# Row flows with ScalarE's copies of older pairs and TensorE's linear layer at the head of each turn

## The chip, the cores and the metric

The kernel runs on one core of a Trainium2 chip. Its engines, TensorE (PE), VectorE (DVE), ScalarE (ACT), GpSimd (POOL) and SyncE (SP, which only issues transfers), each work through their own list of instructions in order and meet at semaphores. The metric is the device time in microseconds of one execution; lower is better. PEclk in the profile is the clock that TensorE was granted, as a share of 2.4 GHz; its other level, 1.2 GHz, reads 0.50.

## The reference

Four layers, each a graph step and a feed-forward step, on x with 2708 rows of 256. What matters here is the beginning of each graph step, which works row by row:

```python
x = x + _L0_gnn_ref(_layernorm(x), adj, L0_gnn_W)     # data = [y, A@y/deg]; data @ W.T
x = x + _L0_ffn_ref(_layernorm(x), ...)               # 32 experts, argmax
x = x + _L1_gnn_ref(_layernorm(x), adj, ...)          # h1 = y @ W1 + b1; three rounds of A @ h
x = x + _L1_ffn_ref(_layernorm(x), ...)               # 8 experts, top 2, weights
x = x + _L2_gnn_ref(_layernorm(x), adj, adj, ...)     # h2 = tanh(y @ W_proj + b); A' @ (h2 @ W_gcn)
# layer 3 and the other feed-forward steps are not touched
```

So before every product with the adjacency matrix each row is normed and multiplied by a 256 x 256 (in layer 0 a 256 x 512) matrix.

## The kernel before, in words

The 2708 rows are padded to 22 tiles of 128, taken as 11 pairs (PR = 11). The three row flows, classes S0, C0 and C1, run the pairs through a chain of steps on several engines. S0 makes [y W] of layer 0 at the program's start; C0 adds the first experts' gathered rows to x and makes the first linear layer of layer 1; C1 adds the weighted rows of the second experts and makes the projection, tanh and second product of layer 2. For each pair:

- VectorE: take (add gathered rows to x, L615 or L657 and L662), statistics (L362), aggregate (L365, semaphore ag);
- ScalarE: root as Ln and Exp (L369, L371, semaphore le; in C1 it is GpSimd's, L375 and L377);
- VectorE: a Newton step, four small instructions (L382 to L390, semaphore rs);
- ScalarE: the two norms (L395, semaphore y);
- TensorE: four transposes (L437, semaphore t);
- ScalarE: high fp16 half (L444, in C1 L747, semaphore xh); VectorE: low half (L412, L785, semaphore xl);
- TensorE: the linear layer in triples of fp16 products (L260 to L262, semaphore mm; in C0 two more for the bias, L577 and L578; in C1 a projection for every second pair first, L756 and L761 its tanh and high half);
- ScalarE: copy of the result as high half HAh (L516, L600 and L603, L766, semaphore hh); VectorE: low half HAl (L531, L628, L775, semaphore hl), in S0 also the residual sum L530 (semaphore xa).

In S0 x itself has to be turned first: TensorE transposes it (L469, semaphore tx) and ScalarE copies it (L502, semaphore xe).

The flows are software pipelines written out by hand: in turn i each engine does step k for pair i - lag(k). The order inside a turn is the order of the lines, and since an engine works in order, an instruction that waits holds up all behind it. Each stage behind a flow begins with work that waits for the flow's last pairs: P0 (L1010 on ScalarE, then L1029 on VectorE), P1 (L881 on TensorE), P2 (L1353 on VectorE). VectorE's order, GpSimd's and SyncE's are the same in both kernels.

Of the kernel before, what the change touches and what calls it, by code (L numbers as in the profile page):

```python
# [14 lines left out]
D = 256  # L15
# [57 lines left out]
def build(nc, io):  # L73
    ctx = ExitStack()
    with ctx:
# [327 lines left out]
        def pair(i):  # L403
            return slice(2 * i, 2 * i + 2)

        def bank2(b):
            return ps[:, b, :].rearrange("p (a d) -> p a d", a=2)
# [40 lines left out]
        class S0:  # L448
# [7 lines left out]
            def pe(self, pe):  # L456
                s = self.st
                w = [z[:, 0:4 * D].rearrange("p (s f d) -> p f s d", s=2, f=FT) for z in (WH, WLo)]
                pe.wait_ge(LC["id"], 16)

                def turn_in(j):
                    for c, (a, b) in enumerate(XCH):
                        if j == a:
                            pe.wait_ge(LC[f"x{c}"], 16)
                    s.wait(pe, "xe", j - 1)
                    for a in range(2):
                        for f in range(FT):
                            q = 2 * a + f
                            mm = pe.transpose(ps[:, 2 + j % 2, q * P:(q + 1) * P],  # L469
                                              xT[:, f, (2 * j + a) * P:(2 * j + a + 1) * P], ident[:, :])  # L470
                    mm.then_inc(s["tx"], 1)

                def linear(j):
                    if j == 0:
                        after(pe, W[0])
                    s.wait(pe, "xl", j + 1)
                    s.wait(pe, "xa", j - 1)
                    s.wait(pe, "hl", j - 1)
                    for a in range(2):
                        out = ps[:, 4 + 2 * (j % 2) + a, :].rearrange("p (s d) -> p s d", s=2)  # L480
                        for f in range(FT):
                            mm = mm3(pe, out, xtp[:, j % 2, 0, 2 * a + f, :], xtp[:, j % 2, 1, 2 * a + f, :],
                                     w[0][:, f], w[1][:, f], start=f == 0, stop=f == FT - 1)
                    mm.then_inc(s["mm"], 1)

                turn_in(0)
                for i in range(PR + 3):
                    if i + 1 < PR:
                        turn_in(i + 1)
                    if 0 <= i - 1 < PR:  # L490
                        turns(pe, s, i - 1, (i - 1) % 2)
                    if 0 <= i - 3 < PR:
                        linear(i - 3)

            def act(self, act):
                s = self.st
                act.preload_act_table_set("natural_log_exp_and_others")
                act.wait_ge(LC["v"], 3)
                for i in range(PR + 4):
                    if i < PR:  # L500
                        s.wait(act, "tx", i + 1)
                        act.activation(x[:, pair(i), :], bank2(2 + i % 2), ACT.Copy).then_inc(s["xe"], 1)  # L502
                        s.wait(act, "ag", i + 1)
                        root_act(act, 2 * (i % 3), 2, s)
                    if i == 1:
                        W[0].act(act)
                    if 0 <= i - 1 < PR:
                        act.wait_ge(s["xe"], s.at("xe") + i)
                        normals(act, s, i - 1)
                    if 0 <= i - 2 < PR:  # L510
                        high_half(act, s, i - 2, (i - 2) % 2)
                    j = i - 4
                    if 0 <= j < PR:
                        s.wait(act, "mm", j + 1)
                        b = 4 + 2 * (j % 2)
                        act.activation(HAh[:, pair(j), 0:D], ps[:, b:b + 2, D:2 * D], ACT.Copy).then_inc(s["hh"], 1)  # L516

            def pool(self, pool):
                W[0].pool(pool)
# [25 lines left out]
        class C0:  # L545
# [18 lines left out]
            def pe(self, pe):  # L564
                s = self.st
                after(pe, self.experts, W[1])
                a0, n0 = _ROWS["L1_b1"]

                def linear(j):
                    s.wait(pe, "xl", j + 1)  # L570
                    s.wait(pe, "hl", j - 1)
                    for a in range(2):
                        out = ps[:, 4 + j % 2, a * D:(a + 1) * D]
                        for f in range(FT):
                            mm3(pe, out, xtp[:, j % 2, 0, 2 * a + f, :], xtp[:, j % 2, 1, 2 * a + f, :],
                                WH[:, f * D:(f + 1) * D], WLo[:, f * D:(f + 1) * D], start=f == 0)
                        pe.matmul(out, ones16[:, 0:P], rowh[:, a0:a0 + n0], start=False, stop=False)  # L577
                        mm = pe.matmul(out, ones16[:, 0:P], rowl[:, a0:a0 + n0], start=False, stop=True)  # L578
                    mm.then_inc(s["mm"], 1)

                for i in range(PR + 3):
                    if 0 <= i - 1 < PR:
                        turns(pe, s, i - 1, 2 + (i - 1) % 2)
                    if 0 <= i - 3 < PR:
                        linear(i - 3)

            def act(self, act):
                s = self.st
                for i in range(PR + 4):
                    if i < PR:  # L590
                        s.wait(act, "ag", i + 1)
                        root_act(act, 2 * (i % 3), 2, s)
                    if 0 <= i - 1 < PR:
                        normals(act, s, i - 1)
                    if 0 <= i - 2 < PR:
                        high_half(act, s, i - 2, 2 + (i - 2) % 2)
                    j = i - 4
                    if 0 <= j < PR:
                        s.wait(act, "mm", j + 1)
                        act.activation(nrow[:, pair(j), :], bank2(4 + j % 2), ACT.Copy).then_inc(s["nn"], 1)  # L600
                        for a in range(2):
                            t = 2 * j + a
                            op = act.activation(HAh[:, t, 0:D], ps[:, 4 + j % 2, a * D:(a + 1) * D], ACT.Identity,  # L603
                                                scale=dinv[:, t:t + 1])
                        op.then_inc(s["hh"], 1)

            def dve(self, v):
                s = self.st
# [58 lines left out]
        class C1:  # L667
# [28 lines left out]
            def pe(self, pe):  # L696
# [26 lines left out]
                    mm.then_inc(s["mm"], 1)  # L723

                for i in range(PR + 8):
                    if 0 <= i - 1 < PR:
                        turns(pe, s, i - 1, 2 + (i - 1) % 2)
                    j = i - 3
                    if 0 <= j < PR and (j % 2 == 1 or j == PR - 1):
                        project(j // 2)  # L730
                    if 0 <= i - 7 < PR:
                        linear(i - 7)

            def act(self, act):
                s = self.st
                after(act, *self.before)
                b0 = _COLS["b_proj"]
                for i in range(PR + 9):
                    if 0 <= i - 1 < PR:
                        normals(act, s, i - 1)  # L740
                    j = i - 2
                    if 0 <= j < PR:
                        g = j // 2
# [6 lines left out]
                    if 0 <= j < PR and (j % 2 == 1 or j == PR - 1):  # L750
# [4 lines left out]
                        for m in range(FT):  # L755
# [4 lines left out]
                        s.wait(act, "mm", 2 * g - 2)  # L760
                        act.activation(self.h2[:, g % 2, 0, :, 0:n, :], self.th[:, :, 0:n * P].rearrange("p m (t c) -> p m t c", c=P),  # L761
                                       ACT.Copy).then_inc(s["h2h"], 1)
                    j = i - 8
                    if 0 <= j < PR:
                        s.wait(act, "mm", j + 1)
                        act.activation(HAh[:, pair(j), 0:D], bank2(6 + j % 2), ACT.Copy).then_inc(s["hh"], 1)  # L766

            def dve(self, v):
                s = self.st
# [1985 lines left out]
```

## Time and profile before

| what | value |
|---|---|
| median of 3 runs | 2637.11 us (2624.55 to 2652.12) |
| the profiled execution's own time | 2658.08 us |
| its span (first to last instruction) | 2655.9 us |
| busy: TensorE, VectorE, ScalarE, GpSimd | 2075.8, 1573.1, 1082.8, 497.0 us |
| mean granted clock of TensorE | 0.895 |
| S0 | 0 to 76 us |
| C0 | first gather issued at 428.35, first take at 437.31, last low half ends at 515.5 |
| C1 | first load issued at 1373.43, first take at 1376.83, last low half ends at 1456.7 |

Busy time is the time in which an engine had an instruction running, and says nothing of why it stood in between. For that the timeline gives, in brackets, how long the engine was idle before an instruction and which instruction's end released it. Instructions on one engine overlap a little: a ScalarE copy that takes 0.58 us lets the next start 0.48 us after its own start, so that lengths of a turn are measured from start to start.

### The profile page before, as it was taken

The numbers are of one execution on the slowest core, as the hardware profiler recorded it, in microseconds if no ns is written. First come the engines' busy times: TensorE is split into PE (matmuls) and PEld (weight loads), VectorE is DVE, ScalarE is ACT, GpSimd is POOL, SyncE is SP. The second block draws the span as 40 slices with busy tenths as digits, with TensorE's granted clock in tenths as the row PEclk, the third lists the DMA queues.
The fourth block names the chain that finished last, engine by engine and source line by source line (L and its number), as shares of the span: only waits on it lengthen the run. The fifth ranks groups of instructions, "written<-read, shape, count | busy, mean of one in ns | idle before, by whom it ended". The sixth has DMA issues, their size and how long they took to land. (4 is left out here: it accounts for less than half of the span.)

```text
span 2655.9 us, 46982 instructions
## 1 busy us (share of the span) xinstructions
PE 2075.8 (78%) x17062; PEld 1393.9 (52%) x17062; DVE 1573.1 (59%) x2950; ACT 1082.8 (41%) x2336; POOL 497.0 (19%) x464
## 2 busy tenths in 40 slices
PE   5899284899999999358856899178954899997597
PEld 3688152588888888346643677166732222222243
DVE  4666654454545566753346897633364899996633
ACT  5454264421212233345534775445543123233344
POOL 0000453000000000374430233544410000000200
PEclk9899597699999999769988899599966999998689
DMA  4899368055455555332223673511230332321000
GB/s 134 256 357 303 103 142 240 15 199 237 198 239 201 238 234 235 109 110 65 65 89 105 168 184 84 160 57 61 67 106 34 125 112 78 90 77 51 16 0 42
DMA packets 211970, 357.69 MB, mean 135 GB/s; under 512 B 18680, under 2 KB 165753, under 8 KB 197050
## 3 DMA queue, kind: packets, MB, share of 16 engines
q1 hardware_dynamic: 189118, 310.39, 34.7%
q0 software_dynamic: 13152, 35.93, 5.2%
q10 hardware_dynamic: 9504, 8.65, 1.0%
q8 instruction: 135, 2.21, 0.3%
q14 instruction: 61, 0.50, 0.1%
HBM read 291.81 MB, written 63.12 MB: 134 GB/s over the span
## 5 line engine op out<-in xcount | busy, mean ns | idle before, releaser
L881 PE MATMUL ps<-R,BIG 128*128 128x256 f16 (+1 forms) x1936 | 532.5, 275 | 23.1 <-DVE BIG L1357 13.4
L882 PE MATMUL ps<-R,BIG 128*128 128x256 f16 x1936 | 528.7, 273 | 0.0
L883 PE MATMUL ps<-R,BIG 128*128 128x256 f16 (+1 forms) x1936 | 528.6, 273 | 0.0
L1799 DVE TENSOR_TENSOR X<-X 128x512 f16<-128x512 f32 (+1 forms) x152 | 84.4, 556 | 332.3 <-ACT X L1780 318.7
L2265 PE MATMUL ps<-BIG 128*64 128x452 f32 x1056 | 233.7, 564 | 35.2 <-DVE BIG L2380 30.8
L881 PEld LDWEIGHTS ps<-R,BIG 128*128 128x128 f16 x1936 | 187.9, 97 | 58.4 <-DVE BIG L1357 13.7
L260 PE MATMUL ps<-X,BIG 128*128 128x128 f16 x904 | 189.6, 227 | 25.3 <-issue 20.0
L882 PEld LDWEIGHTS ps<-R,BIG 128*128 128x128 f16 x1936 | 190.4, 98 | 23.2
L883 PEld LDWEIGHTS ps<-R,BIG 128*128 128x128 f16 x1936 | 188.3, 97 | 26.4
L262 PE MATMUL ps<-X,BIG 128*128 128x128 f16 x904 | 191.0, 227 | 6.6 <-issue 6.5
L261 PE MATMUL ps<-X,BIG 128*128 128x128 f16 x904 | 186.3, 222 | 11.5 <-issue 11.5
L2380 DVE SCALAR_TENSOR_TENSOR BIG<-BIG 128x904 f32<-128x904 f32 x176 | 192.4, 1155 | 4.8 <-DVE BIG L2375 4.0
L1775 ACT ACTIVATE X<-ps,cols 128x128 f32<-128x128 f32 x452 | 137.7, 380 | 126.8 <-PE ps L262 59.6
L2300 ACT ACTIVATE BIG<-X,BIG 128x64 f32 (+1 forms) x264 | 70.2, 337 | 260.8 <-PE ps L2271 260.8
L2265 PEld LDWEIGHTS ps<-BIG 128*64 128x64 f32 x1056 | 64.8, 137 | 201.7 <-issue 119.9
L1676 POOL DMA_INDIRECT X<-rows_split,idxg x152 | 149.7, 985 | 109.3 <-issue 35.4
L1738 PE MATMUL ps<-BIG,X 128*128 x452 | 157.3, 383 | 11.1 <-issue 3.7
L437 PE MATMUL ps<-ident,yln 128*128 128x128 f32 x176 | 42.5, 387 | 123.6 <-ACT yln L395 118.7
L1692 POOL DMA_INDIRECT expert_out<-X,idxs x100 | 98.9, 989 | 188.2 <-DVE X L1805 173.5
L881 PE MATMUL ps<-XX,BIG 128*128 128x256 f16 x484 | 132.2, 273 | 0.3 <-DVE XX L1216 0.3
L883 PE MATMUL ps<-XX,BIG 128*128 128x256 f16 x484 | 131.9, 273 | 0.0
L882 PE MATMUL ps<-XX,BIG 128*128 128x256 f16 x484 | 131.9, 273 | 0.0
(347 smaller groups left out, 4599.7 us busy)
## 6 DMA issues: line engine op xcount, KB each, us to landing
BIG<-adj_split SPq DMA_DIRECT2D x66, 1408.0 KB, 12.8
BIG<-in_adjT SPq DMA_DIRECT2D x42, 1408.0 KB, 11.1
adj_split<-BIG SPq DMA_DIRECT2D x22, 1408.0 KB
BIG<-in_adj SPq DMA_DIRECT2D x22, 1408.0 KB, 6.1
BIG<-in_adjT SPq DMA_DIRECT2D x66, 452.0 KB, 3.3
BIG<-in_f SPq DMA_DIRECT2D x88, 256.0 KB, 3.0
BIG<-expert_out SPq DMA_DIRECT2D x44, 256.0 KB, 2.9
rows_split<-row ACTq DMA_DIRECT2D x66, 128.0 KB, 3.4
```

The source lines that it names most:

```text
L260: pe.matmul(out, ah, bh, start=start, stop=False)
L261: pe.matmul(out, ah, bl, start=False, stop=False)
L262: return pe.matmul(out, al, bh, start=False, stop=stop)
L881: pe.matmul(out[:, 0:n], pr[:, 0, k, :], h[:, k, 0:n], start=start, stop=False)
L882: pe.matmul(out[:, 0:D], pr[:, 0, k, :], l[:, k, 0:D], start=False, stop=False)
L883: return pe.matmul(out[:, 0:n], pr[:, 1, k, :], h[:, k, 0:n], start=False, stop=stop)
L1676: pool.indirect_dma_start(xg[:, j % 4, :], None, xrows[:, :], bass.IndirectOffsetOnAxis(ap=idxg[:, j:j + 1], axis=0)).then_inc(s[f"g{j % 4 ...
L1692: pool.indirect_dma_start(ys_dram[:, :], bass.IndirectOffsetOnAxis(ap=idxs[:, j:j + 1], axis=0), yo[:, j % 4, :], None).then_inc(s[self.ou ...
L1738: pe.matmul(ps[:, 4 + u, :].rearrange("p (h d) -> p h d", h=2), hh[:, u, t, :], w, start=t == 0, stop=False)
L1775: op = act.activation(hact[:, u, t, :], ps[:, 2 + u, t * P:(t + 1) * P], self.func, bias=cols[:, dyn(e[j] * HT + (self.b1 + t), 1)], scale=sc)
L2265: pe.matmul(ps[rs, 2 * (h // 2) + c, 0:CW], self.G[:, u, h * HF:(h + 1) * HF], self.PT[:, u, h, cs], start=start, stop=stop)
L2380: op = v.scalar_tensor_tensor(self.PT[:, u, h, :], Q[h // 2][:, h % 2, :], Z[:, dyn(HEADS * k + h, 1)], self.MK[:, u, :], ALU.max, ALU.mult)
```

## The change

ScalarE's turn is rearranged in all three flows. Before, it did root, norms, high half of pair i-2, then the copy HAh of pair i-4. Now it does the copy HAh, the high half, then the root and the norms; in S0 the copy of x comes first, for pair i+1 in place of pair i, with the copy of pair 0 ahead of the loop. In C1 the copy HAh of pair i-8 is first and the norms are last, behind high half and tanh. TensorE's turn has the linear layer (in C1 projection and linear layer) in front of the transposes of the norms instead of behind them. The lags stay.

```diff
@@ S0.pe
                     if i + 1 < PR:
                         turn_in(i + 1)
+                    if 0 <= i - 3 < PR:
+                        linear(i - 3)
                     if 0 <= i - 1 < PR:
                         turns(pe, s, i - 1, (i - 1) % 2)
-                    if 0 <= i - 3 < PR:
-                        linear(i - 3)
@@ S0.act
+                def rows_in(i):
+                    s.wait(act, "tx", i + 1)
+                    act.activation(x[:, pair(i), :], bank2(2 + i % 2), ACT.Copy).then_inc(s["xe"], 1)
+
+                rows_in(0)
                 for i in range(PR + 4):
+                    if i + 1 < PR:
+                        rows_in(i + 1)
+                    j = i - 4
+                    if 0 <= j < PR:
+                        s.wait(act, "mm", j + 1)
+                        b = 4 + 2 * (j % 2)
+                        act.activation(HAh[:, pair(j), 0:D], ps[:, b:b + 2, D:2 * D], ACT.Copy).then_inc(s["hh"], 1)
+                    if 0 <= i - 2 < PR:
+                        high_half(act, s, i - 2, (i - 2) % 2)
                     if i < PR:
-                        s.wait(act, "tx", i + 1)
-                        act.activation(x[:, pair(i), :], bank2(2 + i % 2), ACT.Copy).then_inc(s["xe"], 1)
                         s.wait(act, "ag", i + 1)
                         root_act(act, 2 * (i % 3), 2, s)
...
-                    if 0 <= i - 2 < PR:
-                        high_half(act, s, i - 2, (i - 2) % 2)
-                    j = i - 4
-                    if 0 <= j < PR:
-                        s.wait(act, "mm", j + 1)
-                        b = 4 + 2 * (j % 2)
-                        act.activation(HAh[:, pair(j), 0:D], ps[:, b:b + 2, D:2 * D], ACT.Copy).then_inc(s["hh"], 1)
@@ C0.pe
+                    if 0 <= i - 3 < PR:
+                        linear(i - 3)
                     if 0 <= i - 1 < PR:
                         turns(pe, s, i - 1, 2 + (i - 1) % 2)
-                    if 0 <= i - 3 < PR:
-                        linear(i - 3)
@@ C0.act (root and norms moved behind; what stands in j's block is unchanged)
-                    if i < PR:
-                        s.wait(act, "ag", i + 1)
-                        root_act(act, 2 * (i % 3), 2, s)
-                    if 0 <= i - 1 < PR:
-                        normals(act, s, i - 1)
-                    if 0 <= i - 2 < PR:
-                        high_half(act, s, i - 2, 2 + (i - 2) % 2)
                     j = i - 4
...
+                    if 0 <= i - 2 < PR:
+                        high_half(act, s, i - 2, 2 + (i - 2) % 2)
+                    if i < PR:
+                        s.wait(act, "ag", i + 1)
+                        root_act(act, 2 * (i % 3), 2, s)
+                    if 0 <= i - 1 < PR:
+                        normals(act, s, i - 1)
@@ C1.pe
-                    if 0 <= i - 1 < PR:
-                        turns(pe, s, i - 1, 2 + (i - 1) % 2)
...
                     if 0 <= i - 7 < PR:
                         linear(i - 7)
+                    if 0 <= i - 1 < PR:
+                        turns(pe, s, i - 1, 2 + (i - 1) % 2)
@@ C1.act
-                    if 0 <= i - 1 < PR:
-                        normals(act, s, i - 1)
+                    j = i - 8
+                    if 0 <= j < PR:
+                        s.wait(act, "mm", j + 1)
+                        act.activation(HAh[:, pair(j), 0:D], bank2(6 + j % 2), ACT.Copy).then_inc(s["hh"], 1)
...
-                    j = i - 8
-                    if 0 <= j < PR:
-                        s.wait(act, "mm", j + 1)
-                        act.activation(HAh[:, pair(j), 0:D], bank2(6 + j % 2), ACT.Copy).then_inc(s["hh"], 1)
+                    if 0 <= i - 1 < PR:
+                        normals(act, s, i - 1)
```

How ScalarE's list stands in the middle of S0 (x is written at X, HAh is R, the high half xt), one turn and the beginning of the next, before:

```order
L369 ACTIVATE nrt<-mvt,eps 128x2
L371 ACTIVATE nrt<-nrt 128x2
L395 ACTIVATE yln<-X,nrt 128x256 x2
L444 ACTIVATE xt<-ps 128x512
L516 ACTIVATE R<-ps 128x2x256
L502 ACTIVATE X<-ps 128x512
```

and in the changed kernel, where L501 is the copy of x and L511 the copy HAh:

```order
L501 ACTIVATE X<-ps 128x512
L511 ACTIVATE R<-ps 128x2x256
L444 ACTIVATE xt<-ps 128x512
L369 ACTIVATE nrt<-mvt,eps 128x2
L371 ACTIVATE nrt<-nrt 128x2
L395 ACTIVATE yln<-X,nrt 128x256 x2
```

Read as a ring the two lists differ only in the order of L444 and the copy HAh. What moved is which pairs meet: the three copies now stand in front of the wait for the aggregate of the turn whose pairs they serve, and the copy of x is one pair ahead.

TensorE's list in S0, with the first linear layer (twelve products in triples, of which the first triple and the last product are shown). Before, the transposes of the norms (L437) of pair 2 stood ahead of it:

```order
L469 MATMUL ps<-ident,X 128x128 x4
L437 MATMUL ps<-ident,yln 128x128 x4
L260 MATMUL ps<-WH,xt 128x512
L261 MATMUL ps<-WLo,xt 128x512
L262 MATMUL ps<-WH,xt 128x512
```

and now, at the second linear layer, they stand behind the products, with the next transposes of x (L469) behind them:

```order
L262 MATMUL ps<-WH,xt 128x512
L437 MATMUL ps<-ident,yln 128x128 x4
L469 MATMUL ps<-ident,X 128x128 x4
L260 MATMUL ps<-WH,xt 128x512
L261 MATMUL ps<-WLo,xt 128x512
```

So L437, which waits for ScalarE's norms, no longer holds up the linear layer of an older pair.

ScalarE's list in C1, a turn without tanh, one with it, and the next norms, in the changed kernel (L747 is now the copy HAh, L754 the high half, L763 tanh, L768 its high half; in the kernel before the norms L395 open a turn and L766, the copy HAh, ends it):

```order
L395 ACTIVATE yln<-X,nrt 128x256 x2
L747 ACTIVATE R<-ps 128x2x256
L754 ACTIVATE XX<-ps 128x2x2x128
L763 ACTIVATE XX<-ps,cols 128x512 x2
L768 ACTIVATE XX<-XX 128x1024
L395 ACTIVATE yln<-X,nrt 128x256 x2
```

The norms of a pair now come behind tanh, which waits for TensorE's projection.

## Rows read from the trace of the kernel before

**Rows 1.** Stretches: us, then each engine's busy us (instructions), PEclk, DMA share, GB/s.
```profile
28.00:60.00 32.00, 21.03 (x113) 11.29 (x110) 19.32 (x66) 17.28 (x41) 0.00 (x0) 1.00 0.06 20
428.00:455.00 27.00, 3.58 (x15) 2.62 (x16) 9.23 (x34) 6.23 (x16) 11.37 (x12) 0.51 0.99 395
455.00:480.00 25.00, 18.67 (x83) 10.01 (x82) 13.02 (x47) 13.14 (x32) 7.57 (x8) 0.57 0.25 83
480.00:507.00 27.00, 21.88 (x92) 11.34 (x90) 14.07 (x47) 12.77 (x30) 1.90 (x2) 0.50 0.04 10
1400.00:1456.00 56.00, 38.47 (x226) 23.89 (x224) 33.05 (x87) 28.88 (x50) 4.73 (x10) 0.84 0.41 106
```

**Rows 2.** Waits in S0, 26 to 76: waiter, releaser, us, times, longest.
```profile
DVE X L530 <- ACT R L516: 22.2, 11, 3.1
```

**Rows 3.** Timeline, one turn of S0: start, us, engine, line, op, [idle before, releaser].
```profile
50.36 0.69 DVE L530 TENSOR_TENSOR X<-X,ps 128x512 f32<-128x512 f32 x1 [2.18 <-ACT R L516]
...
53.09 0.29 ACT L369 ACTIVATE nrt<-mvt,eps 128x2 f32<-128x2 f32 x1 [2.27 <-DVE mvt L365]
...
53.53 0.16 DVE L390 SCALAR_TENSOR_TENSOR nrt<-mvt,nrt 128x2 f32<-128x2 f32 x1
...
53.77 1.09 ACT L395 ACTIVATE yln<-X,nrt 128x256 f32<-128x256 f32 x2 [0.15 <-DVE nrt L390]
...
54.77 0.57 ACT L444 ACTIVATE xt<-ps 128x512 f16<-128x512 f32 x1
...
55.25 0.58 ACT L516 ACTIVATE R<-ps 128x512 f16<-128x512 f32 x1
```

**Rows 4.** Timeline, TensorE in the same turn of S0.
```profile
49.42 0.66 PE L437 MATMUL ps<-ident,yln 128*128 128x128 f32 x4 [1.82 <-ACT yln L395]
...
49.91 0.38 PE L260 MATMUL ps<-WH,xt 128*128 128x512 f16 x1
...
52.50 0.60 PE L469 MATMUL ps<-ident,X 128*128 128x128 f32 x4
```

**Rows 5.** Timeline, S0: first, seventh and last residual sum; ScalarE's next stage.
```profile
28.37 0.69 DVE L530 TENSOR_TENSOR X<-X,ps 128x512 f32<-128x512 f32 x1 [3.15 <-ACT R L516]
...
61.36 0.69 DVE L530 TENSOR_TENSOR X<-X,ps 128x512 f32<-128x512 f32 x1 [2.17 <-ACT R L516]
...
74.84 2.54 ACT L1010 ACTIVATE BIG<-BIG 128x2816 f16<-128x2816 f32 x1
...
74.97 0.69 DVE L530 TENSOR_TENSOR X<-X,ps 128x512 f32<-128x512 f32 x1 [2.05 <-ACT R L516]
```

**Rows 6.** Timeline, one turn of C0.
```profile
473.49 0.88 DVE L628 SCALAR_TENSOR_TENSOR R<-ps,dinv,R 128x256 f16<-128x256 f32 x2 [2.86 <-ACT R L603]
...
476.54 0.29 ACT L369 ACTIVATE nrt<-mvt,eps 128x2 f32<-128x2 f32 x1 [3.09 <-DVE mvt L365]
...
476.97 0.16 DVE L390 SCALAR_TENSOR_TENSOR nrt<-mvt,nrt 128x2 f32<-128x2 f32 x1
...
479.12 0.83 ACT L603 ACTIVATE R<-ps,dinv 128x256 f16<-128x256 f32 x2
...
479.99 0.88 DVE L628 SCALAR_TENSOR_TENSOR R<-ps,dinv,R 128x256 f16<-128x256 f32 x2 [2.86 <-ACT R L603]
```

**Rows 7.** Timeline, C0: takes of gathered rows, pairs 2 and 4.
```profile
446.14 0.69 DVE L615 SCALAR_TENSOR_TENSOR X<-BIG,X 128x512 f32<-128x512 f32 x1 [3.56 <-DMA BIG<-expert_out,posu]
...
454.75 0.69 DVE L615 SCALAR_TENSOR_TENSOR X<-BIG,X 128x512 f32<-128x512 f32 x1 [2.31 <-DMA BIG<-expert_out,posu]
```

**Rows 8.** Timeline, C0: take of the last pair, last low half.
```profile
493.79 0.42 DVE L617 SCALAR_TENSOR_TENSOR X<-BIG,X 128x256 f32<-128x256 f32 x1
...
514.61 0.88 DVE L628 SCALAR_TENSOR_TENSOR R<-ps,dinv,R 128x256 f16<-128x256 f32 x2 [2.67 <-ACT R L603]
```

**Rows 9.** Waits in C1, 1385 to 1460: waiter, releaser, us, times, longest.
```profile
DVE R L775 <- ACT R L766: 20.5, 9, 5.9
```

**Rows 10.** Timeline, the first work of the stage behind C1.
```profile
1456.58 3.08 DVE L1353 SCALAR_TENSOR_TENSOR BIG<-BIG 128x2816 f32<-128x2816 f32 x1
```

## The prediction

> **What bounds the kernel now.** I read the page first for where the time is, then the stretches, then the waits and the timelines of the three flows that are edited: S0 (from the start to 76 us), C0 (428 to 515) and C1 (1373 to 1457). Together they are some 240 of 2656 us; nothing else is touched. In the stretches the reader is to see that no engine is full there: in S0 TensorE is busy for 21.0 of 32 us, VectorE 19.3, ScalarE 17.3; in C0 it is 18.7, 13.0 and 13.1 of 25 [rows 1]. So it is no engine's work that sets the pace but waits in a circle. The waits name it: VectorE stood 22.2 us, all 11 times, for ScalarE's last copy of a turn, L516 [rows 2].
>
> The timeline shows the circle. VectorE's turn opens with the residual sum L530 at 50.36, held until that copy, and ends the part that matters (the aggregate for the root) when ScalarE starts L369 at 53.09: 2.73 us. ScalarE had nothing it could do ahead of this, since the root stands in front of its other work. Then root, norms, and the copies of older pairs follow, L516 from 55.25 to 55.83: 2.74 us [rows 3]. Only now may VectorE's next turn open. 2.73 + 2.74 is 5.47, and the measured turn is (61.36 - 28.37) / 6 = 5.50 us [rows 5]: the two engines run strictly one after the other. C0 is the same: VectorE 473.49 to 476.54 (3.05), ScalarE 476.54 to 479.95 (3.41), turn 6.50 [rows 6].
>
> **The change part by part.** No instruction is added or taken away. Moved are the copies (L516, L444; in S0 also the copy of x one turn ahead) to the head of ScalarE's turn, and TensorE's linear layer in front of the transposes.
>
> *ScalarE's copies first.* The copy that VectorE waits for is now done before ScalarE asks for the next aggregate, so VectorE's turn i can run beside ScalarE's root and norms of turn i-1. The circle above is cut. What is late next is the longest of these, for S0:
> - VectorE's own turn, 50.36 to 53.69: 3.33 us [rows 3].
> - ScalarE's own: root 0.68 (53.09 to 53.77), norms 1.00, three copies at 0.48 start to start: 3.12 us [rows 3].
> - TensorE's own: 2.59 for the linear layer (49.91 to 52.50) and 0.49 for each of two groups of transposes: 3.57 us [rows 4].
> - A new circle through both: ScalarE's turn now opens with the copy of the next x, which waits for its transposes; these stand on TensorE behind the last turn's transposes of the norms; and those wait for ScalarE's norms at the end of its turn. Its length: transposes 0.60 [rows 4], three copies 1.44, root 0.68, norms 1.09 [rows 3], the transposes of the norms 0.49 [rows 4], and three hand-overs that I put at 0.05 each (L516 ends at 55.83; the sum of both halves above leaves 0.03 for one): 4.45 us.
>
> So the S0 turn becomes 4.45, and six turns from 28.37 to 61.36 save 6 x 1.05 = 6.3. In the drain, 61.36 to 74.97 (13.6 for four turns) [rows 5], the transposes of x are over and TensorE's 2.59 + 0.49 = 3.08 is left: 12.3, which saves 1.3. For the filling I take another 1.4, bounded by nothing and a turn and a half. S0: **-9**, bounds -6 and -13.
>
> *TensorE's linear layer first.* Alone it would save nothing: it fills, with work that is ready, the 1.82 us that TensorE stood before L437 [rows 4], and without it the new circle would be longer by 2.59. I count it inside the 4.45.
>
> *C0.* There is no copy of x, so no new circle of that kind. VectorE's own turn is 473.49 to 477.13, 3.64; ScalarE's 3.41 [rows 6]; TensorE's is 18.67 / 25 x 6.50 = 4.85 at the clock of that stretch, 0.57 [rows 1], and some 2.4 at 1.00. Here the clock decides. Between 480 and 507 it is 0.50, the lower level of 1.2 GHz, with a wait before the transposes in each turn; in S0, also with a wait of 1.82 us in each turn, it stays at 1.00, 2.4 GHz [rows 1, 4]. After the change TensorE at the lower level has work for 4.85 in a turn that nothing else holds above 3.64, so it runs without a break, and I expect the upper level after about one turn; then it stands idle 3.64 - 2.4 = 1.2 us in each turn, less than the 1.82 us in S0 at which the upper level held. From the fifth take at 454.75 to the last at 493.79 there are six turns, 39.0 us [rows 7, 8]: one at 4.85 and five at 3.64 make 23.1, saving 16. The drain of 21.7 us behind the last take [rows 8] has five turns; at the upper level ScalarE without the root needs 3.41 - 0.63 = 2.8 for each, 14 together, -7.7; since the clock may rise late, I take half, -4. C0: **-20**, bounds -10 (lower level throughout, six turns of 4.85 = 29.1, drain as now) and -24.
>
> [...]
>
> *The gathers of C0.* Moving VectorE forward asks for gathered rows sooner. The takes of pairs 2 and 4 waited for them, 8.61 us for two turns, 4.3 a turn, while the DMA engines were 99% busy with the next stage's loads up to 455; behind it the share is 0.25 and 0.04 [rows 1, 7]. The loads don't depend on VectorE, so they are over at the same time, and I charge nothing after 455 and gain nothing before.
>
> *C1.* It had the same wait, 20.5 us in 9 times for L766 [rows 9]. In S0 I cut 9 of 22.2. Here ScalarE's tanh, now in front of the norms, waits for TensorE's projection, so part of the wait only moves; I take three tenths: **-6**, bounds 0 and -12.
>
> *What carries on.* S0's end is followed by ScalarE's L1010 at once (74.84) [rows 5], and C1's by VectorE's L1353 at 1456.58 [rows 10]: the stages behind start when the flows end, and so shift whole.
>
> Sum: -9 - 20 - 6 = -35. The profiled execution took 2658.1, so it would be 2623; it is 21 above the median of three, 2637.1, and against the median the forecast is **2602**.
>
> **The rivals.**
> - *The clock stays low in C0 and partly in C1.* C0 -10, C1 -4, S0 -9: -23, 2614. For it: 0.50 through the 27 us from 480 [rows 1]. Against: TensorE had a wait in each turn there, and at the lower level it now has none. 0.20.
> - *The gain is given back behind the flows.* If the stage after S0 is held by its transfers and not by the flow's end, S0's 9 are lost: -26, 2611. Against: L1010 follows at once [rows 5]. 0.12.
> - *Slower: TensorE never gets its clock in S0.* The linear layer and the transposes come in another rhythm; if the clock stayed at 1.2 GHz, TensorE's turn would be 2 x 3.57 = 7.14: six turns 42.8 instead of 33.0, +9.8, and the drain 4 x 6.16 = 24.6 instead of 13.6, +11. C0 -10. C1 had 38.5 busy at a mean clock of 0.84 [rows 1]; all at the lower level that is 38.5 x 0.84 x 2 = 65 in a stretch of 56, +9. Together +20, 2657. It decides from where TensorE's turn at the granted clock passes 5.50, which needs the lower level. Against it: the first linear layers still follow each other closely. 0.08.
>
> That the edit doesn't do what it says is not in question: it is an order written out, and the two orders differ as described.
>
> **How the numbers follow.** The forecast has 0.60, the rivals 0.20, 0.12 and 0.08. Low end: all bounds, -13 - 24 - 12 = -49, 2588, and 8 for the spread of a median (the three runs lie within 2625 to 2652), 2580. High end: the first rival, 2614, and 14 for that spread, 2628. About 1% (26 us) is what a measurement of this kernel can tell from no change. Faster by more than that means under 2611: three quarters of the forecast, half of the next two: 0.60. Slower by more than 1% is most of the last case: 0.06. Within 1%: 0.34.
>
> **What would show it.** In S0: turns of about 4.45 between two residual sums, VectorE's wait for the HAh copy gone, TensorE waiting less than 1 us for the norms, the next stage's first L1010 near 66. In C0: turns near 3.64 and PEclk over 0.9 from about 460; if turns are 4.85 with 0.50, the first rival holds. In C1: the last turns closer, the end 6 us sooner relative to the first take. It would be wrong if the flows shorten and the stages behind them lengthen by as much.

## The result and the profile after

| | before | changed |
|---|---|---|
| median | 2641.41 us (4 runs, 2624.55 to 2652.12) | 2601.06 us (4 runs, 2585.35 to 2605.20) |
| profiled execution, its span | 2658.08, 2655.9 us | 2605.20, 2603.0 us |
| S0, start to end of its last low half | 76.3 us | 61.5 us |
| C0, first take to end of the last low half | 78.2 us | 57.4 us |
| C1, the same | 79.8 us | 73.1 us |

The ratio is 0.983, with a 95% interval from 0.9802 to 0.9857: the changed kernel is 40 us faster. In the profiled executions the three flows together are 14.8 + 20.8 + 6.7 = 42.3 us shorter, and that is where the gain is. The profiled pair differs by 52.9, and the other 10.6 lie in stages that are not edited: 0.8 between S0 and C0, 5.5 between C0's end and C1's first take (861.3 us before, 855.8 after), and 4.3 behind C1. The long stretch between C0 and C1 varies that much by itself: it took 839 to 841 us in each of four kernels on another chip, and on a third chip 838 us in one execution and 856 to 859 us in three others.

S0 in the changed kernel, timeline of one turn (start, us, engine, line, op, [idle before, releaser]). L501 is the copy of x, L511 the copy HAh, L535 the residual sum that was L530; these answer to [rows 3, 4].

```profile
31.96 0.60 ACT L501 ACTIVATE X<-ps 128x512 f32<-128x512 f32 x1 [1.18 <-PE ps L469]
...
32.45 0.59 ACT L511 ACTIVATE R<-ps 128x512 f16<-128x512 f32 x1
...
33.08 0.69 DVE L535 TENSOR_TENSOR X<-X,ps 128x512 f32<-128x512 f32 x1 [0.83 <-ACT R L511]
...
33.41 0.31 ACT L369 ACTIVATE nrt<-mvt,eps 128x2 f32<-128x2 f32 x1
...
33.85 1.08 ACT L395 ACTIVATE yln<-X,nrt 128x256 f32<-128x256 f32 x2
...
34.98 0.66 PE L437 MATMUL ps<-ident,yln 128*128 128x128 f32 x4 [0.47 <-ACT yln L395]
...
35.48 0.60 PE L469 MATMUL ps<-ident,X 128*128 128x128 f32 x4
...
36.11 0.60 ACT L501 ACTIVATE X<-ps 128x512 f32<-128x512 f32 x1 [1.18 <-PE ps L469]
...
37.23 0.69 DVE L535 TENSOR_TENSOR X<-X,ps 128x512 f32<-128x512 f32 x1 [0.83 <-ACT R L511]
```

VectorE's wait of 2.18 us is down to 0.83, and ScalarE's wait for the aggregate (2.27 before L369) is gone. Two other waits now stand in the turn: ScalarE's of 1.18 for the transposes of x, which is new, and 0.47 that is left of TensorE's 1.82 for the norms. They lie on the circle of the forecast, and it can be added up from start to start: L437 to L469 0.50, to L501 0.63, three copies to L369 1.45, to L395 0.44, to L437 1.13, together 4.15. That is the turn.

The waits of S0, 26 to 67, answer to [rows 2], where VectorE's were 22.2 us:

```profile
DVE X L535 <- ACT R L511: 8.0, 9, 1.3
ACT X L501 <- PE ps L469: 5.9, 5, 1.2
PEld ps L437 <- ACT yln L395: 5.8, 6, 1.0
...
PE ps L437 <- ACT yln L395: 2.8, 6, 0.5
```

The first, seventh and last residual sum, and the next stage's first work, for [rows 5]:

```profile
24.77 0.69 DVE L535 TENSOR_TENSOR X<-X,ps 128x512 f32<-128x512 f32 x1 [2.34 <-ACT R L511]
...
48.78 0.68 DVE L535 TENSOR_TENSOR X<-X,ps 128x512 f32<-128x512 f32 x1
...
60.07 2.54 ACT L1015 ACTIVATE BIG<-BIG 128x2816 f16<-128x2816 f32 x1
60.21 0.69 DVE L535 TENSOR_TENSOR X<-X,ps 128x512 f32<-128x512 f32 x1 [1.30 <-ACT R L511]
```

C0, the low halves (L633, was L628) and the last take, for [rows 6 to 8]:

```profile
446.03 0.88 DVE L633 SCALAR_TENSOR_TENSOR R<-ps,dinv,R 128x256 f16<-128x256 f32 x2
...
450.82 0.88 DVE L633 SCALAR_TENSOR_TENSOR R<-ps,dinv,R 128x256 f16<-128x256 f32 x2 [1.14 <-ACT R L601]
...
455.60 0.88 DVE L633 SCALAR_TENSOR_TENSOR R<-ps,dinv,R 128x256 f16<-128x256 f32 x2 [1.14 <-ACT R L601]
...
460.39 0.88 DVE L633 SCALAR_TENSOR_TENSOR R<-ps,dinv,R 128x256 f16<-128x256 f32 x2 [1.14 <-ACT R L601]
...
463.96 0.88 DVE L633 SCALAR_TENSOR_TENSOR R<-ps,dinv,R 128x256 f16<-128x256 f32 x2
464.76 0.41 DVE L622 SCALAR_TENSOR_TENSOR X<-BIG,X 128x256 f32<-128x256 f32 x1
...
467.58 0.87 DVE L633 SCALAR_TENSOR_TENSOR R<-ps,dinv,R 128x256 f16<-128x256 f32 x2
```

The stretches, for [rows 1] (us, busy us of PE, PEld, DVE, ACT, POOL, then PEclk, DMA share, GB/s):

```profile
24.00:46.00 22.00, 19.64 (x108) 10.53 (x106) 16.57 (x56) 15.93 (x39) 0.00 (x0) 1.00 0.31 83
440.00:450.00 10.00, 9.70 (x41) 4.95 (x41) 9.11 (x34) 6.53 (x18) 5.66 (x6) 0.50 0.43 150
450.00:460.00 10.00, 10.00 (x44) 5.50 (x43) 7.02 (x24) 6.79 (x19) 3.78 (x4) 0.50 0.18 52
460.00:465.00 5.00, 5.00 (x37) 3.03 (x34) 4.47 (x15) 4.58 (x13) 0.00 (x0) 0.91 0.10 26
465.00:480.00 15.00, 13.70 (x108) 9.19 (x107) 10.06 (x34) 11.01 (x26) 0.00 (x0) 1.00 0.00 1
```

Here the two views must be read together. Three turns of C0 are 4.79 us long, with TensorE busy all 10.00 us of a stretch at the lower level; the next two are 3.57 and 3.62, with the clock at 0.91 and then 1.00. The lists of instructions are the same in both. What changed is the clock, and with it VectorE's wait of 1.14 for the copy HAh is gone.

C1's waits, 1338 to 1410, answer to [rows 9] (20.5 us there; L780 was L775, L747 was L766), and the start of the stage behind to [rows 10]:

```profile
ACT R L747 <- PE ps L262: 14.7, 7, 4.3
...
DVE R L780 <- ACT R L747: 10.4, 7, 4.2
```

```profile
1407.96 6.08 DVE L1358 SCALAR_TENSOR_TENSOR BIG<-BIG 128x2816 f32<-128x2816 f32 x2
```

### The profile page after: what moved, and what is told of

Read it like the earlier page. It is cut to its first block and busy times, and to the rows that moved or that the text cites. A ratio compares the mean times of both kernels' runs of the same rounds, so it can differ in the third digit from the quotient of the medians.

```text
span 2603.0 us, 46982 instructions
## 1 busy us (share of the span) xinstructions
PE 2067.1 (79%) x17062; PEld 1388.7 (53%) x17062; DVE 1575.1 (61%) x2950; ACT 1080.4 (42%) x2336; POOL 495.7 (19%) x464
## 5 line engine op out<-in xcount | busy, mean ns | idle before, releaser
L886 PE MATMUL ps<-R,BIG 128*128 128x256 f16 (+1 forms) x1936 | 532.5, 275 | 23.1 <-DVE BIG L1362 13.4
L260 PE MATMUL ps<-X,BIG 128*128 128x128 f16 x904 | 189.6, 227 | 17.3 <-issue 11.5
L888 PEld LDWEIGHTS ps<-R,BIG 128*128 128x128 f16 x1936 | 188.3, 97 | 26.3
L2305 ACT ACTIVATE BIG<-X,BIG 128x64 f32 (+1 forms) x264 | 70.2, 337 | 261.3 <-PE ps L2276 261.3
L1743 PE MATMUL ps<-BIG,X 128*128 x452 | 158.4, 383 | 21.1 <-issue 13.3
L2276 PE MATMUL ps<-BIG 128*32 128x452 f32 x1056 | 130.1, 565 | 0.0
```

The lines of the kernel that those rows point to most:

```text
L260: pe.matmul(out, ah, bh, start=start, stop=False)
L886: pe.matmul(out[:, 0:n], pr[:, 0, k, :], h[:, k, 0:n], start=start, stop=False)
L888: return pe.matmul(out[:, 0:n], pr[:, 1, k, :], h[:, k, 0:n], start=False, stop=stop)
L1743: pe.matmul(ps[:, 4 + u, :].rearrange("p (h d) -> p h d", h=2), hh[:, u, t, :], w, start=t == 0, stop=False)
L2276: mm = pe.matmul(ps[32 * h:32 * h + 32, 4 + c, 0:CW], self.G[:, u, z:z + 32], self.PT[:, u, h, cs], start=start, stop=stop)
```

## The experiments

Diffs of the first three are against the kernel before, the others against the changed one. Flow lengths are those of each kernel's own profile, measured as in the table above. Kernels without an interval have one run. Since the stretch between C0 and C1 alone moves a run by some 20 us, the flow lengths carry more than the times of single runs.

### One half alone, one flow alone, and another place for the copy of x

These four ran on one chip, where the kernel before took 2612.23.

**ScalarE's order alone.** Its lists in S0, C0 and C1 as in the changed kernel, TensorE's as before:

```diff
@@ S0.act (C0.act and C1.act in the same way)
+                    if i + 1 < PR:
+                        rows_in(i + 1)
+                    (copy HAh of pair i-4, then the high half of pair i-2)
                     if i < PR:
                         s.wait(act, "ag", i + 1)
                         root_act(act, 2 * (i % 3), 2, s)
```

> ScalarE's order of the changed kernel in all three flows, TensorE's order of the kernel before. Theory (two halves needed in S0): the circle through the transposes of x, 4.15 us in the changed kernel, gets TensorE's linear layer into it, 2.59: S0's turn is 6.7, longer than the 5.50 before, and S0 ends between 80 and 90 instead of 76.3 (before) or 61.5 (changed). C0 has no transposes of x and keeps its gain: about 67 us from the first take to the end as in the changed kernel (421.7 to 479.1 is 57 there, 437.3 to 515.5 is 78 before), so within 3 of the changed one. Rival (ScalarE's order did it all): S0's turn 4.15, its end near 61.5.

Measured 2655.91, 44 slower than the kernel before. S0 ended at 92.6, C0 took 95.9 and C1 91.3. Its timeline, S0 and then C0 (L598, which was L600, copies the linear layer's result as it is, and L601, which was L603, is the scaled copy HAh):

```profile
52.84 0.60 ACT L501 ACTIVATE X<-ps 128x512 f32<-128x512 f32 x1 [3.77 <-PE ps L469]
...
59.58 0.60 ACT L501 ACTIVATE X<-ps 128x512 f32<-128x512 f32 x1 [3.77 <-PE ps L469]
...
62.61 0.66 PE L437 MATMUL ps<-ident,yln 128*128 128x128 f32 x4 [3.06 <-ACT yln L395]
...
482.48 0.60 ACT L598 ACTIVATE X<-ps 128x512 f32<-128x512 f32 x1 [4.95 <-PE ps L583]
...
485.74 1.11 PE L437 MATMUL ps<-ident,yln 128*128 128x128 f32 x4 [3.30 <-ACT yln L395]
...
490.64 0.60 ACT L598 ACTIVATE X<-ps 128x512 f32<-128x512 f32 x1 [4.95 <-PE ps L583]
```

The S0 turn is 6.74 from copy to copy: the measured circle of 4.15 plus the linear layer's 2.59, as priced in the prediction. For C0 the expectation was wrong. There is no copy of x there, but the copies L598 and L601 at the head of the turn wait for the linear layer, which TensorE does behind the transposes, which wait for the norms behind those copies: a circle of 8.16 us at the lower clock, against 6.50 before. So ScalarE's half of the change without TensorE's is a loss in all three flows.

**TensorE's order alone.**

```diff
@@ S0.pe (C0.pe and C1.pe in the same way)
+                    if 0 <= i - 3 < PR:
+                        linear(i - 3)
                     if 0 <= i - 1 < PR:
                         turns(pe, s, i - 1, (i - 1) % 2)
-                    if 0 <= i - 3 < PR:
-                        linear(i - 3)
```

> TensorE's order of the changed kernel in all three flows, ScalarE's order of the kernel before. Theory: the circle of VectorE's and ScalarE's halves is uncut, turns stay 5.50 in S0 and 6.50 in C0, S0 ends at 73 to 76, C0 is at most 3 shorter than before; the span stays within 8 of before. Rival (TensorE's linear layer in front did it): turn 4.15 in S0, end near 61.5.

Measured 2610.29, S0's end at 74.1, turn 5.50, C0 78.8, C1 79.3. TensorE's list by itself changes nothing in the turns; its waits in S0 show that the circle of VectorE and ScalarE is whole:

```profile
DVE X L530 <- ACT R L516: 20.4, 10, 2.2
...
ACT nrt L369 <- DVE mvt L365: 13.6, 6, 2.3
```

**Both halves, in S0 alone.** The diff is the S0 part of the change.

> Both orders changed in S0 alone, C0 and C1 as before. Theory (the flows add up, and what S0 gains is carried whole): S0 ends at 61.5, all up to C0's first take is 14.7 earlier, C0 and C1 are as long as before (78.2 and 79.9 from first take to end). Rival (a shorter S0 only meets the next stage's transfers sooner, or changes the clock behind it): part of the 14.7 is gone at C0's first take.

Measured 2598.83: 13.4 less, S0's end at 62.3, turn 4.15. C0 and C1 had about their old lengths (76.5 and 80.0). A difference of 13.4 between two single runs proves little by itself, but the profiles of this kernel and of the one with TensorE's order alone, on the same chip, can be followed stage by stage: S0 ends 11.8 us sooner (62.3 against 74.1), C0's first take comes 13.3 sooner (421.2 against 434.5), and the whole span is 11.5 shorter. So what S0 gains is kept to the end.

**The copy of x last.** This breaks the new circle at its other end: the copy no longer stands in front of root and norms.

```diff
@@ S0.act
                 for i in range(PR + 4):
-                    if i + 1 < PR:
-                        rows_in(i + 1)
...
                     if 0 <= i - 1 < PR:
                         normals(act, s, i - 1)
+                    if i + 1 < PR:
+                        rows_in(i + 1)
```

> The changed kernel with S0's copy of the next x at the end of ScalarE's turn instead of its head. Theory: S0's turn of 4.15 is the circle transposes of x, copies, root, norms, transposes; with the copy of x behind the norms the norms don't wait for the transposes of x, and what is left is TensorE's own 3.57 or VectorE's own 3.33 plus a hand-over: turn 3.6 to 3.9, S0 ends at 57 to 60. Rival (VectorE's statistics now wait for the late copy of x, a new circle of VectorE and ScalarE): turn 4.15 or more.

Measured 2564.40, S0's end at 59.8 and the steady turn 3.82. The timeline shows a shorter circle, VectorE's statistics for the late copy of x:

```profile
35.67 0.68 DVE L535 TENSOR_TENSOR X<-X,ps 128x512 f32<-128x512 f32 x1
...
36.84 0.57 ACT L501 ACTIVATE X<-ps 128x512 f32<-128x512 f32 x1
...
37.44 0.75 DVE L362 BATCH_NORM_STATS2 bst<-X 128x6 f32<-128x256 f32 x2 [0.49 <-ACT X L501]
...
39.49 0.68 DVE L535 TENSOR_TENSOR X<-X,ps 128x512 f32<-128x512 f32 x1
```

That moving one copy takes 0.33 from each turn shows that the copy's place was part of the circle. Of the 34 us to the kernel of S0 alone, 20 are C0 (56.3 against 76.5), 7 are C1 (72.9 against 80.0) and 2 are S0; the other 5 lie in stages that neither edits.

### C0's clock, and C1's norms

These four ran on a second chip, where the kernel before took 2649.67.

**The changed kernel again.**

> The changed kernel once more, on the chip of the three runs beside it, as what they are compared with. Theory: the flows have the same lengths as in its first profile (S0 ends at 61.5, C0 57.8 and C1 73.1 from first take to end), and TensorE's clock in C0 rises near the same place. Rival: where the clock rises in C0 is chance, and C0's length differs by more than 3 us.

Measured 2605.52. S0 ended at 61.8 and C1 took 71.7, as before; C0 took 53.6 in place of 57.4, since the clock rose earlier, as the rival of this expectation had it:

```profile
440.00:450.00 10.00, 8.68 (x51) 5.00 (x49) 7.91 (x26) 7.23 (x18) 3.89 (x5) 0.79 0.61 224
450.00:460.00 10.00, 8.22 (x59) 4.52 (x56) 9.59 (x36) 9.42 (x25) 5.58 (x6) 1.00 0.24 68
```

Its turns are 3.56 from 444.60 on. The upper level came to stay at about 461 us in the first profile of this program, at 448 in this one and at 453 in a third (the changed kernel, timed, below). So what C0 gains has a part of about 4 us that is not the kernel's.

**C0 without the bias.** The bias b1 is left out of C0's linear layer (the two products with a row of ones that add it), so that TensorE has less to do.

```diff
@@ C0.pe
-                        pe.matmul(out, ones16[:, 0:P], rowh[:, a0:a0 + n0], start=False, stop=False)
-                        mm = pe.matmul(out, ones16[:, 0:P], rowl[:, a0:a0 + n0], start=False, stop=True)
```

> The changed kernel without the two bias products of each row tile in C0 (the linear bias b1 of layer 1's graph step is left out). They stand for some 1.3 us of TensorE's 4.79 at the lower clock. Theory (TensorE at 1.2 GHz is what holds C0's turns of 4.79): four turns between 442 and 461 fall to VectorE's own 3.64, C0 is 3 to 5 shorter than 57.8. Rival (the turn of 4.79 is another circle of the three engines): turns stay within 0.3 of 4.79.

Measured 2595.05, C0 52.7, turns 3.75 and then 3.57:

```profile
440.00:450.00 10.00, 5.16 (x38) 3.61 (x38) 8.43 (x27) 7.65 (x19) 4.31 (x5) 0.98 0.58 211
450.00:460.00 10.00, 5.93 (x47) 4.30 (x46) 9.59 (x36) 9.20 (x23) 5.15 (x6) 1.00 0.27 72
```

The clock was up here before C0's steady turns began, so the expectation's question, whether less work at the lower level shortens the turn of 4.79, was not put. What the run does show: over a quarter less of TensorE's work (5.93 us of 10 in place of 8.22) moves the turn by nothing once the clock is up. VectorE, busy 9.59 of 10, is the limit. And the clock holds at 1.00 with TensorE idle 4.07 of 10 us.

**More work for TensorE, early.** 36 products into an unused bank in three turns of C0.

```diff
@@ C0.pe
+                    if 2 <= i <= 4:
+                        for _ in range(12):
+                            pe.matmul(ps[:, 7, :], one2[:, :], WH[:, 0:512], start=True, stop=True)
```

> The changed kernel with 36 products more in C0 (ones times W, 512 columns, into an unused bank, read by nobody), 12 ahead of the third, fourth and fifth turn, where TensorE waited for gathered rows. Theory (the lower clock costs C0 four turns of 4.79 instead of 3.64, and work in the gaps brings the upper level before the steady turns): turns of 3.64 from 446 on, C0 shorter by 3 to 5. Rival (the added work delays the first linear layers by more than the clock gives back): C0 the same or longer, by up to 8.

Measured 2602.12, C0 54.6. The clock is up from 440 on, but one turn of its low halves is 4.87, with TensorE full of the added products, and only then come turns of 3.56:

```profile
444.81 0.87 DVE L636 SCALAR_TENSOR_TENSOR R<-ps,dinv,R 128x256 f16<-128x256 f32 x2
...
449.68 0.87 DVE L636 SCALAR_TENSOR_TENSOR R<-ps,dinv,R 128x256 f16<-128x256 f32 x2
...
453.24 0.87 DVE L636 SCALAR_TENSOR_TENSOR R<-ps,dinv,R 128x256 f16<-128x256 f32 x2
```

The added work cost as much as the clock gave: C0 is 1 us longer than in the changed kernel beside it, whose clock also rose early.

**C1's norms in front of tanh.**

```diff
@@ C1.act
+                    if 0 <= i - 1 < PR:
+                        normals(act, s, i - 1)
                     (high half and tanh)
-                    if 0 <= i - 1 < PR:
-                        normals(act, s, i - 1)
```

> The changed kernel with C1's norms ahead of tanh again (behind the copy HAh and the high half). Theory (C1's gain of 6.8 comes from the copy HAh ahead of all; norms behind tanh cost a part, since TensorE waits some 2.6 us for them in every second turn): C1 is 1 to 4 shorter than 73.1. Rival (TensorE's wait costs nothing, and tanh later makes the second product late): C1 0 to 3 longer.

Measured 2601.33, C1 70.2 against 71.7. TensorE's wait for the norms, summed from 1338 to 1410, falls from 33.2 in the changed kernel beside it to 27.0. The longest, 16.4, stands in both: it is the wait for the flow's first norms. This kernel's:

```profile
PE ps L437 <- ACT yln L395: 27.0, 7, 16.4
```

One pair of runs would not be enough for 1.5 us, since C1 took 71.5 to 74.2 in the seven profiles that have the changed kernel's C1. But the three with the norms in front, this one and two below, took 70.2, 70.0 and 67.6, all under that range. So part of what C1 did not gain stood behind tanh.

### Orders that the runs pointed to

These four ran on a third chip, where the kernel before had a median of 2640.73 (7 runs).

**The high half behind the norms,** in S0 and C0.

```diff
@@ S0.act (C0.act in the same way)
-                    if 0 <= i - 2 < PR:
-                        high_half(act, s, i - 2, (i - 2) % 2)
...
                     if 0 <= i - 1 < PR:
                         normals(act, s, i - 1)
+                    if 0 <= i - 2 < PR:
+                        high_half(act, s, i - 2, (i - 2) % 2)
```

> The changed kernel with ScalarE's copy of the high half at the end of its turn again in S0 and C0; the copy HAh, the copy of x and TensorE's order stay as changed. Theory (it is the copy HAh ahead of the root that cuts the old circle, and each copy ahead of the norms lengthens the new one by its 0.48): S0's turn is 4.15 less 0.48, 3.67, or TensorE's own 3.57 to 3.8, and S0 ends at 58 to 61; C0 within 2 of the changed one. Rival (VectorE's low half, which comes before its aggregate, needs the high half early as well): the old circle is back, turn near 5.5 in S0 and 6.5 in C0.

Measured 2604.20 in one run, S0's end at 59.5. The steady turn is near 3.70; one of 3.67, from the residual sums:

```profile
32.23 0.69 DVE L535 TENSOR_TENSOR X<-X,ps 128x512 f32<-128x512 f32 x1 [0.39 <-ACT R L511]
...
35.90 0.69 DVE L535 TENSOR_TENSOR X<-X,ps 128x512 f32<-128x512 f32 x1 [0.31 <-ACT R L511]
```

One of three copies went out of the circle, and the turn went down by 0.45, near the copy's 0.48. In C0 the same move is a loss: at the upper level its turns are 3.91, against 3.56 in the changed kernel, and it took 57.0 against 55.0 in the changed kernel on this chip. There VectorE's low half L412 now waits for the high half L444, 3.5 us in 8 times from 440 to 477.

**The changed kernel, timed.**

> The changed kernel, timed beside the kernel before in rounds. Theory (S0 -14.7, C0 -21 to -24, C1 -7 to -8, nothing elsewhere): ratio 0.982 to 0.986. Rival (a part of the first comparison was chance between chips): 0.988 or more.

Median 2599.03 (5 runs, 2580.64 to 2605.59), ratio 0.985 with an interval from 0.9798 to 0.9899. S0's end 62.9, C0 55.0, C1 73.5.

**The copy of x last in S0, and the norms in front of tanh in C1.** The two diffs above together.

> The changed kernel with S0's copy of x at the end of ScalarE's turn (S0 1.7 shorter in its run) and C1's norms ahead of tanh (C1 1.5 shorter in its run). Theory (both add): S0 ends near 60, C1 near 70, together 3 us less than the changed kernel beside it, a ratio to before lower by 0.001. Rival: no difference or longer, one of the two being chance of the clock.

Median 2592.76 (4 runs, 2589.86 to 2597.66), ratio 0.982 with an interval from 0.9769 to 0.987. S0's end 60.9, C0 53.6, C1 70.0: the flows are 1.9, 1.4 and 3.5 us shorter than in the changed kernel beside it, and the medians differ by 6.3. Only C1's part is clear. C0 is not edited here, and its clock rose 7 us sooner. Of S0's 1.9 only 0.5 lie in the six turns (23.5 against 24.0); the rest is the filling, and the first residual sum comes anywhere from 24.8 to 26.3 in kernels with the changed kernel's S0. The intervals overlap, so the time does not settle it. It has the lowest median of the three versions timed on this chip.

**High half, then x, both last.**

```diff
@@ S0.act (C0.act with the high half alone; C1's norms in front of tanh)
                     if 0 <= i - 1 < PR:
                         normals(act, s, i - 1)
+                    if 0 <= i - 2 < PR:
+                        high_half(act, s, i - 2, (i - 2) % 2)
+                    if i + 1 < PR:
+                        rows_in(i + 1)
```

> As the run before it, and with the copy of the high half at the end too, in S0 and C0 (ScalarE's turn: HAh, root, norms, high half, and in S0 the next x). Theory: nothing but root and norms lie on the circle through TensorE, S0's turn is TensorE's own 3.57 and S0 ends at 57 to 60; total 3 to 6 us under the changed kernel. Rival (high half at the end brings back the circle with VectorE's low half): turn over 4.5, total longer than the changed kernel.

Median 2598.46 (4 runs, 2593.24 to 2604.79), no better than the changed kernel. The S0 turn is 4.30, and in one case 4.63:

```profile
35.47 0.58 ACT L501 ACTIVATE X<-ps 128x512 f32<-128x512 f32 x1
...
36.08 0.75 DVE L362 BATCH_NORM_STATS2 bst<-X 128x6 f32<-128x256 f32 x2 [0.97 <-ACT X L501]
...
37.61 0.30 ACT L369 ACTIVATE nrt<-mvt,eps 128x2 f32<-128x2 f32 x1 [1.04 <-DVE mvt L365]
...
38.62 1.09 ACT L395 ACTIVATE yln<-X,nrt 128x256 f32<-128x256 f32 x2 [0.47 <-DVE nrt L390]
...
39.61 0.57 ACT L444 ACTIVATE xt<-ps 128x512 f16<-128x512 f32 x1
40.09 0.58 ACT L501 ACTIVATE X<-ps 128x512 f32<-128x512 f32 x1
```

The expected turn failed. Each of the two moves shortens the S0 turn alone. Together they bring x so late that VectorE waits 0.97 for it, and ScalarE then 1.04 for the aggregate. It is not the circle of the kernel before, which went through the copy HAh, but that of the run with the copy of x last, now with the high half in it: 3.82 + 0.48 = 4.30. In the turn shown it is 0.61 + 1.53 + 1.01 + 0.99 + 0.48 = 4.62, with 0.47 more of waiting for L390. Against the changed kernel on this chip S0 ends 1.4 later (64.2), C0 is 4.5 longer (59.5, with turns of 3.91 and a clock that fell back) and C1 5.9 shorter (67.6, norms in front of tanh), which adds up to nothing.

## Why the prediction was right, step by step

The median, 2601.06, stands beside the forecast of 2602, and the forecast's own mechanism came about. That the two agree to 1 us is luck. The forecast was a gain of 35 from a median of 2637; the measured gain is 40.4, and with its fourth run the median of the kernel before is 4.3 higher. Not all terms have the right size, and some offset each other.

- **What bounds the kernel before**: right. ScalarE's order with TensorE's breaks the circle VectorE-ScalarE; TensorE's order alone leaves it at 5.50.
- **"Without it the new circle would be longer by 2.59"**: right, 6.74 - 4.15. The prediction priced this for S0 only. That C0 has a like circle through the copies L598 and L601 was not seen there, nor in the first expectation.
- **S0, -9 with bounds -6 and -13**: mis-sized, and outside its own bounds: -14.8. The new circle has the parts that were named, but is 4.15 and not 4.45. Most of this 0.30 is the root: 0.68 was read from L369 to L395 in [rows 3], and this held a wait for VectorE's L390, which ran there until 53.69. Now the norms find that result ready and follow after 0.44. All other parts together were off by 0.06. The first and the seventh residual sum lie 24.0 apart in place of 33.0, -9.0 against -6.3: 1.5 of the 2.7 come from the shorter circle, and 1.2 from the last of the six turns, which has no transposes of x and is 3.24. The drain gave -2.2 (13.6 to 11.4) against -1.3. The filling gave -3.6 (28.37 to 24.77), where 1.4 was taken without a row; this is the term furthest off, and part of it is chance, since the first residual sum came at 27.2 in the kernel with TensorE's order alone and at 24.8 to 26.3 in kernels with the changed S0.
- **C0, -20**: right in sum, -20.8, by parts that offset. The six turns were 25.4 in place of 39.0, so -13.6 against -16: at least three turns were at the lower level where one was expected. The drain gave -7.4, which is the -7.7 that the prediction halved in case the clock rose late. In the second execution of the changed kernel the clock did rise early, and C0 was 24.6 shorter than the 78.2 of before, just past the forecast's bound of -24.
- **C0's clock**: the turns are 3.57 at the upper level and 4.79 at the lower, against 3.64 and 4.85. The 4.85 was read over a stretch with a mean clock of 0.57; over 480 to 507, at 0.50, the same reading gives 21.88 / 27 x 6.50 = 5.3, so its closeness is luck in part. The first rival, that the clock stays low, fell: PEclk is 1.00 from 465 to 480 and stays there with TensorE idle 1.3 of 15 us. In the kernel without the bias it stays with 4.07 of 10 idle. The Trainium skill's page "TensorE: Matmul & The Clock Gate", section "HAM oscillation — how this bites in real kernels", describes short groups of matmuls with DMA waits of about 3 to 5 us between them, each group starting at half rate. No run here tests that: in the kernel before, TensorE's waits for the norms were 1.47 to 2.26 us in S0 at 1.00 and 1.65 to 2.35 in C0, mostly at 0.50, so waits of about one size stood at both levels. TensorE's own turn at the upper level was put at 2.4, where its own rows give 4.85 x 0.57 = 2.8; it is 8.22 / 10 x 3.56 = 2.9, still under VectorE's.
- **The gathers**: right in effect, with a wrong reason. The loads are not over at the same time: from 440 to 450 the DMA share is 0.43 against 1.01 before, so they came forward with the end of S0. From C0's first take to its fifth it is 17.7 us (421.71 to 439.36), against 17.4 before, so nothing was gained or lost there, and no take behind the fifth waited for rows.
- **C1, -6**: right in size, -6.7, but only a share of a wait and no circle worked out, then or since. VectorE's wait fell from 20.5 to 10.4. Half of that wait went and not three tenths, and part of it only moved, as the prediction had it: ScalarE now waits 14.7 us for TensorE before L747.
- **What carries on**: right. With S0 alone changed, 11.8 us at S0's end were 11.5 at the end of the span, and the second rival fell.
- **The slower rival**, TensorE's clock down in S0: fell. PEclk is 1.00 from 24 to 46, TensorE busy 19.64 of 22.
- **The conversion to the median**: 21 us between the profiled execution and the median were carried over unchanged. The profiled pair differs by 52.9 and the medians by 40.4; the flows' 42.3 fits the medians.

What is left open: what decides in which turn of C0 the clock rises. Three executions of one program differ in it, and no edit here moved it for certain without a cost of its own. Nor does it only rise: with the high half and x last it was 1.00 from 455 to 465, with TensorE busy 8.05 of the 10 us, and then 0.51 from 465 to 475, while in the kernel without the bias it held at 5.93 of 10. C1's circle is open too. And the 838 to 861 us of the untouched stage were seen, not explained.

## What to carry to other kernels

When engines that work through lists in order take turns, draw the circle from start to start and add up its parts; the turn is the longest circle, and an edit is worth its difference to the next longest one. Two lists have to be moved together where each holds a step that the other's head waits for: ScalarE's list alone made the three flows some 45 us longer here, TensorE's alone did next to nothing, and both gave 40. Take each part of the new circle without the waits that stood inside it before, since these belong to the old one.

## What the runs showed of the hardware

- TensorE ran without a break for the 10 us from 450 to 460 at 1.2 GHz in one execution of the changed kernel (10.00 us busy, PEclk 0.50), and in another was at 2.4 GHz in the same stretch with 8.22 us busy (PEclk 1.00).
- In the kernel without the bias the upper level held through turns in which TensorE was idle for 41% of the time (5.93 busy of 10, PEclk 1.00). In the kernel with the high half and x last it was lost behind a stretch with 8.05 busy of 10.
- A stretch of some 860 us that no edit touched took 838 to 861 us, and on one chip alone 838 in one execution and 856 to 859 in three others. That is half of what the change gives: flow lengths told these kernels apart where single times did not.
